# Attention outputs placed by feature with DMAs and divided late, in a two-layer kernel on one Trainium2 core

## Chip, cores and metric

The kernel runs on one core of a Trainium2 chip. The metric is the device time of one execution in microseconds (us), median of the runs shown. The engines are named as in the profile: PE (TensorE matmul; PEld its weight loads), DVE (VectorE), ACT (ScalarE), POOL (GpSimd) and SP (SyncE, here a queue that only issues DMAs and waits). All inputs and the output are float32.

## The reference, cut to what matters

The input has 2 sequences of 1024 tokens with 128 features. Two layers follow each other: attention plus a state scan with a mixture of experts, then a causal latent attention with a second mixture of experts. Both attentions have 16 heads of 8 features. What is computed around the change is, for each head:

```python
# layer 0, full attention (4 key/value heads, one for each group of 4 query heads)
p = softmax(q @ k.T / sqrt(8)); out = p @ v             # out: tokens x 8, 16 heads side by side = 128 features
# layer 1, causal
attn = jnp.where(causal_mask[None, None], -jnp.inf, attn)
attn = jax.nn.softmax(attn, axis=-1)
y = jnp.einsum('bhtl,hld->bhtd', ctx, v_eff).transpose(0, 2, 1, 3).reshape(B, T, C)
x = x + y                                               # the residual
```

The softmax's denominator is the row sum of the exponentials. The kernel computes numerators (exponentials times v) and denominators (exponentials times one) and divides afterwards.

## The kernel before

Activations are held by feature: 128 features on the partitions, 2048 tokens in the free direction, as four blocks of 512 columns. The program is a chain of blocks with a barrier between: preparation of the scan, attention 0 (`hybrid_attention`, profile 90 to 515 us), the scan (515 to about 1170 us), `latent_layer` (merge, gated layer and experts of layer 0, and attention 1, whose units run from 1320 to 1575 us), and the experts of layer 1 to the end. A block ends when each of its engines has come to its end.

Both attentions are the one function `attention`. A unit is one group of 4 heads of one sequence; there are 8 units (`UNITS`), in the order given by `units`. In a unit the queries are in two halves `qb` of 512. It has NE slots, 32 in attention 0 and 24 in attention 1; a slot handles one tile of 128 keys for two heads: PE computes their transposed scores (`exp_unit`), ACT takes the exponential of two 128x512 tiles (in attention 1 they are cut by the causal mask), and PE multiplies with v (`pv_quad`), into one bank `out_acc`. The rows of `out_acc` are 32 for each head: 8 numerators, one denominator (the column of ones in `vst`), and 23 unused. Half 0 ends with slot MID - 1 (MID is 16 in attention 0 and 8 in attention 1).

Beside that a first pass runs ahead in the same slots: PE computes scores (`max_unit`), DVE takes their row maxima (`take_max`, L581 in attention 0, L578 in attention 1), `combine` splits the maxima in three bf16 parts (L591 to L595), PE turns them to rows (`turn_max`), ACT copies the rows (L514), and SP's `rows` places them with three DMAs (L310, the tile `attn_mrow`) in the query operand `attn_qa`. The exponentials of half 0 of unit i wait for `rows(i, 0)`, those of half 1 for `rows(i, 1)` (`mrow_sent`). The planner's slots (worked out from its code) are: attention 0, `turn_max(i, 1)` in slot 12 for slot 16, `turn_max(i + 1, 0)` in slot 28 for slot 0 of the next unit; attention 1, `turn_max(i, 1)` in slot 3 for slot 8, `turn_max(i + 1, 0)` in slot 12 for slot 0 of the next unit. In the last unit there is no unit ahead, so the first pass ends early (slot 10 of attention 0, slot 1 of attention 1).

SP also loads the operands of unit i + 2 (`load_part`, three parts of six DMAs, L266 and L299), each paced by a wait on a slot of unit i. In attention 0 SP ends with `sync_third`, which loads 3.5 MB for the scan back into SBUF (ct, bt and twelve pieces of xparts) and waits for them; before, it comes right after the last `rows(7, 1)`.

When a half is done, the output goes: ACT copies `out_acc` to SBUF (`out_copy`, L519, tile `attn_osb`); PE turns it to token-major in 32 weight loads and 32 matmuls (`turn_out`, L362 with `attn_osb`, into the bank `turned`); DVE takes the reciprocal of 16 denominators per token row and multiplies (`out_norm`, L604 and L608), into a token-major buffer that is `ssm_in`. `turn_out(i - 1, 1)` stands in slot 3 (attention 0) or 5 (attention 1) of unit i (`OUT_AT`), `turn_out(i, 0)` in slot MID + 3. After the last unit PE turns the whole buffer back to features (L503, 4 x 4 tiles of 128x128), and ACT copies it to `attn_t` (attention 0, L563) or DVE adds it to x (attention 1, L638).

Of the kernel before, what the change touches and what calls it, by code (L numbers as in the profile page):

```python
# [14 lines left out]
T = BATCH * SEQ  # L15
# [117 lines left out]
def sl(i, w=BLK):  # L133
    return slice(i * w, (i + 1) * w)
# [6 lines left out]
def attention(k, tag, q_lin, k_lin, k_heads, v, causal, attn_t, front, units, tok=None, residual=False,  # L141
# [18 lines left out]
    with ExitStack() as ctx:  # L160
# [8 lines left out]
        osb = k.sb(f"{tag}_osb", [128, BLK], F32, ctx)  # L169
        rden = k.sb(f"{tag}_rden", [128, 4, 4], F32, ctx)  # L170
        if tok is None:
            tok = k.sb(f"{tag}_tok", [128, T], F32, ctx)
        attn_tok = tok[:, :].rearrange("p (t m) -> p t m", m=HEADS * HD)
# [56 lines left out]
        OUT_AT = 5 if causal else 3  # L230
# [17 lines left out]
        oturned = k.sem(f"{tag}_oturned")  # L248
        normed = k.sem(f"{tag}_normed")
        own_dve = k.sem(f"{tag}_own_dve")  # L250
        own_norm = k.sem(f"{tag}_own_norm")
        final_turned = k.sem(f"{tag}_final_turned")
        final_copied = k.sem(f"{tag}_final_copied")
# [15 lines left out]
        with nc.Block() as block:  # L269
            @block.sync  # L270
            def _(sp):
# [40 lines left out]

                front.sync_first(sp, load_part)
# [8 lines left out]
                for i in range(UNITS):  # L322
                    rows(i, 1)
                    if i + 2 < UNITS:
                        load_part(i + 2, 0)
                    if causal and i + 1 < UNITS:
                        rows(i + 1, 0)
                    if i + 2 < UNITS:
                        load_part(i + 2, 1)
                        load_part(i + 2, 2)  # L330
                    if not causal and i + 1 < UNITS:
                        rows(i + 1, 0)
                front.sync_third(sp)

            @block.gpsimd
            def _(pool):
# [9 lines left out]
                for i in range(2):  # L346
                    nc.gpsimd.memset(vst[i][:, :, :, :], 0.0).then_inc(vst_cleared, 1)
                    pool.wait_ge(vst_cleared, 2 * i + 1)
                    nc.gpsimd.memset(vst[i][:, :, :, HD:HD + 1], 1.0).then_inc(vst_cleared, 1)
# [5 lines left out]
            def _(pe):  # L355
# [23 lines left out]
                def turn_max(i, half):  # L379
# [3 lines left out]
                    if i > 0:  # L383
                        pe.wait_ge(normed, 2 * i - 1 + (half if not causal else 0))
                    if causal and half == 1:
                        pe.wait_ge(mrow_ready[0], i + 1)
                    for t in range(4):
# [45 lines left out]
                def turn_out(i, qb):  # L433

                    pe.wait_ge(osb_ready, 2 * i + qb + 1)
                    pe.wait_ge(normed, 2 * i + qb)

                    if qb == 0:
                        pe.wait_ge(mrow_ready[1], i + 1)
                    elif i + 1 < UNITS:  # L440
                        pe.wait_ge(mrow_ready[1 if causal else 0], i + 2)
                    for t in range(4):
                        last = quad(turned[:, sl(t, TILE)], osb[:, sl(t, TILE)], k.m("ident"))
                    last.then_inc(oturned, 1)

# [8 lines left out]
                def body(i):  # L454
                    for s in range(NE):
# [22 lines left out]
                        if s == OUT_AT and i > 0:  # L478
                            turn_out(i - 1, 1)
                        if s == MID + 3:  # L480
                            turn_out(i, 0)
# [14 lines left out]
                turn_out(UNITS - 1, 1)  # L496

                pe.wait_ge(normed, 16)
                for n in range(NBLK):
                    if n >= 2:  # L500
                        pe.wait_ge(final_copied, n - 1)
                    for t in range(4):
                        last = nc.tensor.matmul(k.bank[n % 2][:, sl(t, TILE)], attn_tok[:, 4 * n + t, :],  # L503
                                                k.m("ident"), start=True, stop=True)
                    last.then_inc(final_turned, 1)
# [2757 lines left out]
```

## Time and profile before

| | us |
|---|---|
| median of 3 runs | 1913.33 (1907.16 to 1920.68) |
| profiled execution | 1904.06 |
| its span | 1902.3 |
| PE busy over the span | 1624.3 (85%) |
| DVE busy | 1478.2 (78%) |
| ACT busy | 1350.6 (71%) |
| POOL busy | 882.9 (46%) |

All times of the rows below are from the start of the span of the profiled execution. A busy share is an average over stages with different limits; what matters here is which engine has no gap in the two attentions, and what follows what where they end.

### The profile page before, as it was taken

How to read it: one execution, taken by the hardware profiler on the slowest of the kernel's cores; microseconds unless marked ns; L12 is line 12 of the kernel's file. 1: busy time of each engine (PE TensorE's matmuls, PEld its weight loads, DVE VectorE, ACT ScalarE, POOL GpSimd, SP SyncE). 2: the span in 40 equal slices, each digit the busy share in tenths (PEclk: the TensorE clock that was granted, in tenths of full speed). 3: DMA queues.
4: the chain of work that ended last, by engine and by line, in shares of the span. 5: the costliest groups of instructions: out<-in, count | busy, mean ns of one | idle time of the engine just before them, and what ended most of it. 6: DMA issues, size and time to landing. Idle time of an engine off the chain costs nothing. (4 is left out here: it accounts for less than half of the span.)

```text
span 1902.3 us, 45877 instructions
## 1 busy us (share of the span) xinstructions
PE 1624.3 (85%) x17422; PEld 857.2 (45%) x17422; DVE 1478.2 (78%) x1729; ACT 1350.6 (71%) x2673; POOL 882.9 (46%) x526
## 2 busy tenths in 40 slices
PE   6789999999887766676767669998999998999996
PEld 2235555555344434344444433433556555344442
DVE  3588899999299999999999975447888845556457
ACT  4418888888799999989999953443777773654443
POOL 0166666666099999999999971000000002000000
PEclk8769999999999899898888989996999999999998
DMA  2344444443489988888898842031222100000000
GB/s 118 119 154 151 161 154 159 158 155 136 142 325 313 319 309 299 313 289 306 295 319 300 299 148 88 13 72 41 46 39 46 30 4 18 0 1 0 0 6 17
DMA packets 82504, 278.86 MB, mean 147 GB/s; under 512 B 11159, under 2 KB 11954, under 8 KB 81311
## 3 DMA queue, kind: packets, MB, share of 16 engines
q1 hardware_dynamic: 68223, 225.67, 35.7%
q0 software_dynamic: 13824, 50.34, 6.7%
q8 instruction: 124, 2.03, 0.5%
q10 hardware_dynamic: 288, 0.45, 0.1%
q14 instruction: 45, 0.37, 0.1%
HBM read 214.72 MB, written 61.21 MB: 145 GB/s over the span
## 5 line engine op out<-in xcount | busy, mean ns | idle before, releaser
L1680 POOL TENSOR_TENSOR hc<-st,ct 128x1024 f32<-128x1024 f32 x256 | 596.5, 2369 | 9.8 <-DVE st L1626 8.4
L1626 DVE TENSOR_TENSOR_SCAN st<-da,banks 128x1024 f32<-128x1024 f32 x256 | 561.9, 2265 | 13.5 <-ACT da L1583 5.5
L528 ACT ACTIVATE attn_probs<-banks 128x512 f32<-128x512 f32 (+3 forms) x640 | 325.0, 534 | 91.3 <-PE banks L362 74.6
L362 PE MATMUL banks<-attn_qa,attn_ka 75*32 75x512 bf16 (+3 forms) x3584 | 346.7, 363 | 9.3 <-DMA attn_qa<-attn_mrow 2.9
L581 DVE TENSOR_REDUCE attn_mx<-banks 128x1 f32<-128x1024 f32 x256 | 309.9, 1223 | 29.0 <-PE banks L362 16.7
L1591 ACT ACTIVATE ut<-b_turned,mats 128x128 f32<-128x128 f32 x1024 | 311.7, 388 | 1.7
L362 PE MATMUL banks<-attn_ka,attn_qa 72*32 72x512 bf16 (+3 forms) x3584 | 289.5, 379 | 17.5 <-DVE attn_mx L578 10.8
L1583 ACT ACTIVATE da<-dt,mats 128x1024 f32<-128x1024 f32 x256 | 282.7, 1139 | 22.6 <-DVE st L1626 17.4
L1508 PE MATMUL banks<-hc,onecols 128*32 128x512 f32 x1024 | 155.9, 686 | 95.5 <-POOL hc L1680 73.8
L759 POOL TENSOR_TENSOR made_ahead<-b_turned,x_turned 128x1024 f32<-128x1024 f32 x96 | 184.2, 1918 | 89.4 <-DVE attn_mparts L595 70.8
L578 DVE CUSTOM_DVE_ANT_0 banks<-banks,attn_maskwide 128x128 f32<-128x128 f32 (+7 forms) x256 | 191.2, 775 | 31.4 <-PE banks L362 27.8
L1483 PE MATMUL banks<-mats,ut 128*128 128x128 f32 x1024 | 167.3, 300 | 45.7 <-DVE st L1626 34.8
L425 PE MATMUL banks<-attn_probs,attn_vst 128*32 128x256 f32 (+3 forms) x2560 | 180.2, 349 | 1.6 <-ACT attn_probs L528 0.5
L528 ACT ACTIVATE centred_squares<-banks 128x512 f32<-128x512 f32 x256 | 150.6, 596 | 37.0 <-PE banks L362 27.4
L1483 PEld LDWEIGHTS banks<-mats,ut 128*128 128x128 f32 x1024 | 132.5, 150 | 83.7 <-ACT ut L1591 53.4
L362 PEld LDWEIGHTS banks<-attn_qa,attn_ka 75*32 75x32 bf16 x3584 | 101.0, 94 | 133.1 <-ACT attn_probs L528 47.4
L362 PEld LDWEIGHTS banks<-attn_ka,attn_qa 72*32 72x32 bf16 x3584 | 108.0, 99 | 96.3 <-DVE attn_mx L578 23.8
L2627 PE MATMUL banks<-hid_m,ew 128*128 128x512 f32 x320 | 146.4, 592 | 0.0
L1491 PEld LDWEIGHTS banks<-mats,ua 128*128 128x128 f32 x768 | 98.7, 160 | 104.9 <-issue 60.1
L1491 PE MATMUL banks<-mats,ua 128*128 128x128 f32 x768 | 124.0, 314 | 8.0 <-DVE st L1626 7.8
L3066 POOL MEMSET route_tok<- 128x128 bf16 x1 | 0.2, 205 | 272.9 <-issue 272.9
L425 PEld LDWEIGHTS banks<-attn_probs,attn_vst 128*32 128x32 f32 x2560 | 78.3, 110 | 33.7 <-issue 4.2
(447 smaller groups left out, 1938.5 us busy)
## 6 DMA issues: line engine op xcount, KB each, us to landing
dt<-dt_rows SPq DMA_DIRECT2D x256, 512.0 KB, 5.6
ahead<-made_ahead POOLq DMA_DIRECT2D x96, 512.0 KB, 3.3
ua<-ahead SPq DMA_DIRECT2D x96, 512.0 KB, 6.0
attn_qa<-q_lin SPq DMA_DIRECT2D x144, 64.0 KB
attn_ka<-k_lin SPq DMA_DIRECT2D x72, 64.0 KB
moe_w<-in_moe_w SPq DMA_DIRECT2D x2, 2048.0 KB, 9.8
mats<-in_mats SPq DMA_DIRECT2D x1, 2988.5 KB, 13.0
xparts_kept<-xparts_lin SPq DMA_DIRECT2D x3, 512.0 KB, 4.7
```

The source lines that it names most:

```text
L362: last = nc.tensor.matmul(out[sl(t, 32), :], lhs[:, sl(t, 32)], rhs, start=start, stop=True, skip_group_check=True)
L425: last = nc.tensor.matmul(out_acc[32 * j:32 * j + 32, cols], vstage[:, kt, kj(j), :], probs[(kt_slot + j // 2) % 4][:, j % 2, cols],  star ...
L528: nc.scalar.activation(probs[s % 4][:, jj, c0:BLK], scores_exp[jj][:, c0:BLK], ACT.Exp, scale=scale).then_inc(probs_ready, 1)
L578: nc.vector.tensor_tensor_reduce(out, out, mask_wide[:, SEQ - w:SEQ], 1.0, -BIG, ALU.add, ALU.max, mx[:, qt, j:j + 1]).then_inc(max_taken, 1)
L581: nc.vector.reduce_max(mx[:, qt, j:j + 1], out, AX.X).then_inc(max_taken, 1)
L759: nc.gpsimd.tensor_tensor(stage[:, :, :], scan.b_turned[:, 8 * b:8 * b + 8, :], x, ALU.mult)\
L1483: ins = nc.tensor.transpose(pair[:, i // 4, sl(i % 4, TILE)], buf[:, i, :], k.m("ident"))
L1491: ins = nc.tensor.transpose(pair[:, i // 4, sl(i % 4, TILE)], ua[q % 3][:, i, :], k.m("ident"))
L1583: nc.scalar.activation(da[n % 4][:, :], dt[n % 4][:, :], ACT.Exp, scale=a_now[:, g, jp:jp + 1])\
L1591: nc.scalar.activation(ut[TURNED.index(n) % 2][:, i, :], b_turned[:, 8 * b + i, :], ACT.Copy, scale=x_now[:, i, g, jp:jp + 1]).then_inc(ut ...
L1626: nc.vector.tensor_tensor_scan(st[n % 4][:, :], da[n % 4][:, :], pair[:, :, :].rearrange("p h t -> p (h t)"), 0.0, ALU.mult, ALU.add).then ...
L1680: nc.gpsimd.tensor_tensor(hc[n % 8][:, :], st[n % 4][:, :], ct[:, b * SEQ:(b + 1) * SEQ], ALU.mult)\
```

## The change

The turned output is gone: no `turn_out`, no `out_norm`, no token-major buffer, no final turning, and no `rden`.

- `vst` now has ones in 8 columns per head and not in one, so `out_acc` has per head 8 numerators and 8 equal denominators on 16 of its 32 rows.
- `out_copy` writes one of two buffers `osb[qb]`, and waits only for the DMAs that read this buffer one unit earlier (`out_sent[qb]`).
- SP's new `out_rows(i, qb)` waits for the copy and issues 8 DMAs of 8 partitions x 512 float32: for each of the 4 heads, numerators to `attn_t` and denominators to `den_t` (the same memory as the token-major buffer before, `ssm_in`). So there are 16 more DMAs for each unit on SP's queue.
- In attention 0 the order of SP in iteration i is: `out_rows(i-1, 1)`, `rows(i, 1)`, `load_part(i+2, 0)`, `out_rows(i, 0)`, `load_part(i+2, 1)`, `load_part(i+2, 2)`, `rows(i+1, 0)`. In attention 1 it is: `rows(i, 1)`, `out_rows(i-1, 1)`, `load_part(i+2, 0)`, `out_rows(i, 0)`, `rows(i+1, 0)`, `load_part(i+2, 1)`, `load_part(i+2, 2)`. After the last unit `out_rows(7, 1)` comes ahead of `sync_third`.
- DVE's new `divide(b, qb)` works on a whole block of 128x512 by feature: a reciprocal in place, a multiplication, and in attention 1 the addition to x. The two blocks of the sequence that is finished first are divided from slot 12 of the last unit on, the third from slot MID + 7, the fourth after the last `out_rows` has landed.
- `turn_max` waits for ACT's copy of the rows before (`mrow_ready`) where it waited for DVE's `normed`.

```diff
--- before.py
+++ after.py
...
@@ -166,11 +166,7 @@
         mrow = k.sb(f"{tag}_mrow", [12, 2, BLK], BF16, ctx)
-        osb = k.sb(f"{tag}_osb", [128, BLK], F32, ctx)
-        rden = k.sb(f"{tag}_rden", [128, 4, 4], F32, ctx)
-        if tok is None:
-            tok = k.sb(f"{tag}_tok", [128, T], F32, ctx)
-        attn_tok = tok[:, :].rearrange("p (t m) -> p t m", m=HEADS * HD)
+        osb = [k.sb(f"{tag}_osb{i}", [128, BLK], F32, ctx) for i in range(2)]
         ident_b = k.sb(f"{tag}_identb", [128, 128], BF16, ctx)
@@ -227,7 +223,6 @@
         turn_at = [done_half[0] + 2, done_half[1] + 2]
-        OUT_AT = 5 if causal else 3
         LOAD_SLOT = [5, 14, 18] if causal else [13, 19, 23]
...
@@ -310,6 +303,17 @@
+                def out_rows(i, qb):
+
+                    g, b = units[i]
+                    cols = slice(b * SEQ + qb * BLK, b * SEQ + (qb + 1) * BLK)
+                    sp.wait_ge(osb_ready, 2 * i + qb + 1)
+                    for j in range(4):
+                        rows = sl(4 * g + j, HD)
+                        sp.dma_start(attn_t[rows, cols], osb[qb][32 * j:32 * j + HD, :]).then_inc(out_sent[qb], 16)
+                        sp.dma_start(den_t[rows, cols], osb[qb][32 * j + HD:32 * j + 2 * HD, :])\
+                            .then_inc(out_sent[qb], 16)
+
                 front.sync_first(sp, load_part)
@@ -320,9 +324,14 @@
                 for i in range(UNITS):
+                    if i > 0 and not causal:
+                        out_rows(i - 1, 1)
                     rows(i, 1)
+                    if i > 0 and causal:
+                        out_rows(i - 1, 1)
                     if i + 2 < UNITS:
                         load_part(i + 2, 0)
+                    out_rows(i, 0)
                     if causal and i + 1 < UNITS:
@@ -330,6 +339,7 @@
                         rows(i + 1, 0)
+                out_rows(UNITS - 1, 1)
                 front.sync_third(sp)
@@ -346,7 +356,7 @@
                     pool.wait_ge(vst_cleared, 2 * i + 1)
-                    nc.gpsimd.memset(vst[i][:, :, :, HD:HD + 1], 1.0).then_inc(vst_cleared, 1)
+                    nc.gpsimd.memset(vst[i][:, :, :, HD:2 * HD], 1.0).then_inc(vst_cleared, 1)
                     pool.wait_ge(vst_cleared, 2 * i + 2)
@@ -380,10 +390,10 @@
-                    if i > 0:
-                        pe.wait_ge(normed, 2 * i - 1 + (half if not causal else 0))
-                    if causal and half == 1:
+                    if half == 1:
                         pe.wait_ge(mrow_ready[0], i + 1)
+                    elif i > 0:
+                        pe.wait_ge(mrow_ready[1], i)
                     for t in range(4):
@@ -429,19 +439,6 @@
                         last.then_inc(pv_done, 2)
-
-                def turn_out(i, qb):
-
-                    pe.wait_ge(osb_ready, 2 * i + qb + 1)
-                    pe.wait_ge(normed, 2 * i + qb)
-
-                    if qb == 0:
-                        pe.wait_ge(mrow_ready[1], i + 1)
-                    elif i + 1 < UNITS:
-                        pe.wait_ge(mrow_ready[1 if causal else 0], i + 2)
-                    for t in range(4):
-                        last = quad(turned[:, sl(t, TILE)], osb[:, sl(t, TILE)], k.m("ident"))
-                    last.then_inc(oturned, 1)
@@ -475,10 +472,6 @@
                             pv_quad(*products_with_v, 1)
-                        if s == OUT_AT and i > 0:
-                            turn_out(i - 1, 1)
-                        if s == MID + 3:
-                            turn_out(i, 0)
@@ -493,16 +486,6 @@
                     pv_quad(UNITS - 1, NE - 2, vst[1], part)
-                turn_out(UNITS - 1, 1)
-
-                pe.wait_ge(normed, 16)
-                for n in range(NBLK):
-                    if n >= 2:
-                        pe.wait_ge(final_copied, n - 1)
-                    for t in range(4):
-                        last = nc.tensor.matmul(k.bank[n % 2][:, sl(t, TILE)], attn_tok[:, 4 * n + t, :],
-                                                k.m("ident"), start=True, stop=True)
-                    last.then_inc(final_turned, 1)
@@ -515,8 +498,9 @@
                     act.wait_ge(pv_done, NE * i + half_end[qb] + 1)
-                    act.wait_ge(oturned, 2 * i + qb)
-                    nc.scalar.copy(osb[:, :], out_acc[:, :]).then_inc(osb_ready, 1)
+                    if i > 0:
+                        act.wait_ge(out_sent[qb], 128 * i)
+                    nc.scalar.copy(osb[qb][:, :], out_acc[:, :]).then_inc(osb_ready, 1)
@@ -558,9 +542,6 @@
                 out_copy(UNITS - 1, 1)
-                for n in range(NBLK if not residual else 0):
-                    act.wait_ge(final_turned, n + 1)
-                    nc.scalar.copy(attn_t[:, sl(n)], k.bank[n % 2][:, :]).then_inc(final_copied, 1)
@@ -596,18 +577,21 @@
-                def out_norm(i, qb):
-
-                    dve.wait_ge(oturned, 2 * i + qb + 1)
-                    dve.wait_ge(normed, 2 * i + qb)
-                    tv = turned[:, :].rearrange("p (t j c) -> p t j c", t=4, j=4)
-                    link(nc.vector.reciprocal(rden[:, :, :], tv[:, :, :, 8]), 2 * i + qb + 1, own_norm)
-                    g, b = units[i]
-                    t0 = b * QT + 4 * qb
-                    dst = attn_tok[:, t0:t0 + 4, sl(g, 32)].rearrange("p t (j c) -> p t j c", j=4)
-                    nc.vector.tensor_tensor(dst, tv[:, :, :, 0:8],
-                                            rden[:, :, :].unsqueeze(3).to_broadcast([128, 4, 4, 8]), ALU.mult)\
-                        .then_inc(normed, 1)
+                def divide(b, qb):
+
+                    unit = max(i for i, u in enumerate(units) if u[1] == b)
+                    blk = 2 * b + qb
+                    dve.wait_ge(out_sent[qb], 128 * (unit + 1))
+                    num, den = attn_t[:, sl(blk)], den_t[:, sl(blk)]
+                    taken[0] += 1
+                    link(nc.vector.reciprocal(den, den), taken[0], inverted)
+                    ins = nc.vector.tensor_tensor(num, num, den, ALU.mult)
+                    if residual:
+                        link(ins, taken[0], divided)
+                        nc.vector.tensor_tensor(k.x[:, sl(blk)], k.x[:, sl(blk)], num, ALU.add)
+
+                taken = [0]
+                last_b = units[UNITS - 1][1]
@@ -618,10 +602,10 @@
                                 combine(i + 1, 0)
-                        if s == OUT_AT and i > 0:
-                            out_norm(i - 1, 1)
-                        if s == MID + 3:
-                            out_norm(i, 0)
+                        if i == UNITS - 1 and s in (12, 13):
+                            divide(1 - last_b, s - 12)
+                        if i == UNITS - 1 and s == MID + 7:
+                            divide(last_b, 0)
@@ -632,11 +616,7 @@
                     body(i)
-                out_norm(UNITS - 1, 1)
-                for n in range(NBLK if residual else 0):
-                    dve.wait_ge(final_turned, n + 1)
-                    nc.vector.tensor_tensor(k.x[:, sl(n)], k.x[:, sl(n)], k.bank[n % 2][:, :], ALU.add)\
-                        .then_inc(final_copied, 1)
+                divide(last_b, 1)
```

## Rows read from the trace of the kernel before

**Rows 1.** Busy time by stretch (stretch, length, PE, PEld, DVE, ACT, POOL, clock, DMA share, GB/s)
```profile
200.00:250.00 50.00, 49.02 (x924) 29.61 (x920) 45.56 (x50) 43.29 (x76) 31.91 (x26) 1.00 0.41 152
...
1400.00:1450.00 50.00, 48.03 (x1228) 28.84 (x1217) 43.69 (x117) 37.99 (x84) 0.00 (x0) 1.00 0.28 43
```

**Rows 2.** Timeline of PE in unit 1 of attention 0 (start, us, instruction, idle before)
```profile
195.29 1.08 PE L362 MATMUL banks<-mats,attn_osb 128*32 128x128 f32 x32
196.16 0.43 PE L362 MATMUL banks<-attn_qa,attn_ka 75*32 75x512 bf16 x4
...
206.25 0.40 PE L362 MATMUL banks<-attn_ka,attn_qa 72*32 72x512 bf16 x4 [0.54 <-DVE attn_mx L581]
```

**Rows 3.** Timeline of DVE in the same stretch
```profile
196.43 0.26 DVE L604 RECIPROCAL attn_rden<-banks 128x16 f32<-128x16 f32 x1 [0.32 <-PE banks L362]
196.72 0.29 DVE L608 TENSOR_TENSOR ssm_in<-banks,attn_rden 128x128 f32<-128x128 f32 x1
197.06 9.05 DVE L581 TENSOR_REDUCE attn_mx<-banks 128x1 f32<-128x1024 f32 x7
```

**Rows 4.** Timeline of attention 1, unit 1: PE and SP's queue
```profile
1354.68 0.27 PE L388 MATMUL banks<-attn_identb,attn_mparts 128*12 128x128 bf16 x2
...
1356.18 1.81 SPq L310 DMA_DIRECT2D attn_qa<-attn_mrow  x3
...
1357.58 1.04 PE L362 MATMUL banks<-mats,attn_osb 128*32 128x128 f32 x32
...
1360.02 0.40 PE L362 MATMUL banks<-attn_qa,attn_ka 75*32 75x512 bf16 x4
```

**Rows 5.** Timeline of attention 0, unit 0 into unit 1: ACT, SP's queue, PE
```profile
169.92 0.58 ACT L519 COPY attn_osb<-banks 128x512 f32<-128x512 f32 x1
...
185.89 1.89 SPq L310 DMA_DIRECT2D attn_qa<-attn_mrow  x3
...
189.79 0.40 PE L362 MATMUL banks<-attn_qa,attn_ka 75*32 75x512 bf16 x4 [0.34 <-DMA attn_qa<-attn_mrow]
```

**Rows 6.** Instructions by line (count: duration in ns, min/median/max, first and last start)
```profile
L299 SPq DMA_DIRECT2D attn_qa<-q_lin x144: 263/298/1432, 97.5 to 1504.3; - x144
...
L310 SPq DMA_DIRECT2D attn_qa<-attn_mrow x96: 572/578/772, 137.8 to 1546.0; - x96
...
L604 DVE RECIPROCAL attn_rden<-banks x32: 256/258/259, 173.5 to 1569.1; 128x16 f32<-128x16 f32 x32
...
L595 DVE TENSOR_TENSOR attn_mparts<-attn_mres,attn_mparts x32: 174/176/177, 136.4 to 1543.3; 128x16 bf16<-128x16 f32 x32
```

**Rows 7.** Timeline of the end of attention 0 and the start of the scan
```profile
485.34 0.45 SPq L732 DMA_DIRECT2D ct<-ct_kept  x1
...
507.82 0.59 ACT L519 COPY attn_osb<-banks 128x512 f32<-128x512 f32 x1 [1.19 <-PE banks L425]
...
515.02 0.35 SPq L1461 DMA_DIRECT2D dt<-dt_rows  x1
```

**Rows 8.** Busy time by stretch there, columns as in rows 1
```profile
495.00:500.00 5.00, 4.58 (x72) 1.68 (x76) 0.00 (x0) 4.62 (x10) 0.00 (x0) 1.00 0.90 181
500.00:505.00 5.00, 4.65 (x76) 1.53 (x68) 0.00 (x0) 4.70 (x10) 0.00 (x0) 1.00 0.01 4
515.00:519.00 4.00, 3.49 (x14) 1.79 (x14) 0.17 (x1) 2.94 (x12) 0.00 (x0) 1.00 0.63 219
519.00:522.40 3.40, 0.00 (x0) 0.00 (x0) 2.15 (x1) 1.71 (x2) 0.00 (x0) 1.00 1.02 388
522.60:529.00 6.40, 5.39 (x21) 3.87 (x21) 5.87 (x4) 6.40 (x17) 4.96 (x5) 0.50 1.03 409
```

**Rows 9.** Timeline of the end of attention 1 and what follows
```profile
1567.34 0.59 ACT L519 COPY attn_osb<-banks 128x512 f32<-128x512 f32 x1 [0.55 <-PE banks L425]
...
1573.79 0.69 DVE L638 TENSOR_TENSOR x<-x,banks 128x512 f32<-128x512 f32 x1 [0.21 <-PE banks L503]
1574.76 0.30 SPq L3092 DMA_DIRECT2D alpha<-in_eb_rows  x1
1574.80 3.67 PE L2509 MATMUL banks<-x,mats 128*128 128x512 f32 x8 [1.04 <-PEq L269]
```

More of the change, by code:

```diff
@@ L138, with attention @@
 K_ORDER = [0, 1, 2] * 3
-def attention(k, tag, q_lin, k_lin, k_heads, v, causal, attn_t, front, units, tok=None, residual=False,
+def attention(k, tag, q_lin, k_lin, k_heads, v, causal, attn_t, front, units, den_t, residual=False,
               probs=()):
@@ L247, in attention @@
         osb_ready = k.sem(f"{tag}_osb_ready")
-        oturned = k.sem(f"{tag}_oturned")
-        normed = k.sem(f"{tag}_normed")
+        out_sent = [k.sem(f"{tag}_out_sent{i}") for i in range(2)]
         own_dve = k.sem(f"{tag}_own_dve")
-        own_norm = k.sem(f"{tag}_own_norm")
-        final_turned = k.sem(f"{tag}_final_turned")
-        final_copied = k.sem(f"{tag}_final_copied")
+        inverted = k.sem(f"{tag}_inverted")
+        divided = k.sem(f"{tag}_divided")
         vst = [k.sb(f"{tag}_vst{i}", [128, QT, nk, 32], F32, ctx) for i in range(2)]
```

## The prediction

> **What bounds the kernel now.** I read the busy time by stretch first, since only the two attentions are touched. In both, PE is busy 48 to 49 of 50 us, DVE 44 to 46, ACT 38 to 43, at full clock [rows 1]. Busy PE can be overlapping records, so the second view is PE's timeline around a turned output. There `turn_out` starts at 195.29 and the next scores at 196.16: it takes 0.87 us of PE's stream, and the work before and behind it stands without a gap [rows 2]. The third view is DVE at the same place: it waits 0.32 us for the turning, spends 0.63 us on `out_norm` (196.43 to 197.06), and then takes seven maxima in 9.05 us, 1.29 each, where PE delivers one a slot [rows 3]. PE's next wait for DVE is 0.54 us at 206.25, ten microseconds later and at a `combine` [rows 2]. So PE sets the pace, and DVE makes up its delay.
>
> Two more places matter. Where a half's exponentials begin, PE may wait for the max rows: three DMAs, issued from 185.89 to 187.78, let PE on at 189.79, so they land 2.0 us after their issue, and PE had waited 0.34 us [rows 5]. And each attention has an end in which one thing follows another: the last output copy, turning, norm, final turning, final copy [rows 7, 9].
>
> **In the units.** There are 32 outputs (the count of L604 [rows 6]): 15 in each attention beside other work, and one at each end.
>
> Attention 0: no `turn_out` lies between a `turn_max` and the slot that needs its rows (12 to 16, 28 to 0; the outputs are in slots 3 and 19). So each gives back its 0.87 us: 15 x 0.87 = 13.1 us saved.
>
> Attention 1: the output of slot MID + 3 = 11 lies free: 8 x 0.87 = 7.0 us saved. That of slot 5 lies inside the chain from `turn_max` in slot 3 to slot 8: turned at 1354.68, rows issued 1356.18 to 1357.99, plus 2.0 us = 1360.0, and slot 8 starts at 1360.02 [rows 4]. PE would be there 0.87 us earlier and wait for the same DMAs. What is late next is the max rows, and the stall that goes comes back whole. I take nothing for these seven; the other bound is 7 x 0.87 = 6.1 us.
>
> DVE's 0.63 us an output go too. They bring nothing more as long as PE sets the pace; a bound for the case that they do is among the rivals. ACT's copy is the same. The ones in 8 columns cost nothing: the matmul has 32 columns per head anyway.
>
> **On SP's queue.** 16 DMAs a unit come in. A price for this form is not in the trace. The load of 8 partitions (L299) takes SP 0.30 us, the small one from SBUF to SBUF (L310) 0.58 [rows 6]; three of these take 1.81 to 1.89 [rows 4, 5], so there is 0.04 between. The new ones have 8 partitions on both sides and equal shapes, nearest to L299: 0.34 apiece, 2.7 us for eight; the other bound is 0.61, 4.9 us. Behind `out_rows(i, 0)` two parts of loads (12 x 0.34 = 4.1 us) and `rows(i+1, 0)` are queued, whose lateness PE feels at once (it waits already). The copy is done at 170.50 and those rows are issued at 185.89 [rows 5]: 15.4 us for 4.9 + 4.1 at most. Hidden. `out_rows(i-1, 1)` starts near slot 2, ten slots ahead of `rows(i, 1)`; in attention 1 it stands behind it. ACT's wait for `out_sent` looks one unit back, 30 us or more: nothing.
>
> **The end of attention 0.** Before: copy done at 508.41, scan starts at 515.02, 6.6 us [rows 7]. `sync_third` began at 485.34 [rows 7], and its transfers filled the DMA engines until 500 (share 0.90, then 0.01 [rows 8]): 14.7 us, hidden under unit 7. Now it is queued behind `out_rows(7, 1)`, which waits for the last copy. So nothing hides it: 2.7 + 14.7 + 0.3 for leaving the block = 17.7 us, 11.1 us lost. This is the step that a look at PE alone misses. If the transfers held the rate of their first megabytes, they would take some 10 us (bound 6 lost); with 0.61 a DMA 13.3 are lost. DVE's last division runs beside.
>
> **The end of attention 1.** Before: copy done 1567.93, next stage 1574.76, 6.8 us [rows 9]. Now: 2.7 of issue, 2.0 to land, reciprocal, multiplication 0.69, addition 0.69, 0.1 between, 0.3 to leave. The reciprocal of 128x512 is not in the trace. That of 16 elements takes 258 ns where a TENSOR_TENSOR of 16 takes 176 [rows 6], and one of 512 takes 690 [rows 9], so the latter is 1.04 ns an element on 160 ns. If the rest of the reciprocal is per element, it is 98/16 = 6.1 ns, 3.3 us for 512. Bounds: 0.8 us (the 82 ns are fixed), 8.3 us (all 258 ns scale). I take 3.3, between them, for the extra over a TENSOR_TENSOR is large for so few elements. Sum 9.8 us, 3.0 lost (0.5 to 8, or 2.2 more with slow DMAs).
>
> The Trainium skill (VectorE: DVE Perf Modes, "First, the fixed hardware budget") says that the reciprocal is an iterative divide with a repeat count of 8. At its 0.96 GHz an estimate from that is 4.3 us, 1 us more than by the row; no row here shows a long one. The three earlier divisions of each attention lie where DVE has no maxima left.
>
> **The clock.** PE was idle from 519.0 to 522.4, and the granted clock of the next stretch is 0.50, that is 1.2 GHz [rows 8]. After the change PE is idle for 18 and 10 us at the two ends, where before it was turning. The scan then begins with 3.5 us of PE work at full clock in its first 4 us [rows 8], the experts with 3.67 us for eight matmuls [rows 9]. At half clock each takes up to 3.5 us more. In the scan PE shares the path with the first loads: 1.5 us; the experts start on PE: 2.0 us; bounds 0 and 3.5 each.
>
> The Trainium skill (TensorE: Matmul & The Clock Gate, "Part 1") speaks against this change for the same reason: an idle array falls back to half rate and must earn the full one again. It agrees with the row; without it the sum would be 3.5 us lower.
>
> **Sum.** -13.1 - 7.0 + 11.1 + 3.0 + 1.5 + 2.0 = -2.5 us. Against the profiled execution's 1904.06 that is 1901.6. The median of the runs shown is 9 us above that execution, so on its scale 1913.3 - 2.5 = 1910.8. About 1% (19 us) is what a measurement can tell from no change.
>
> **Rivals.**
> A. Both engines' stalls add up (faster). If PE's 0.87 and DVE's 0.63 us come back one behind the other in all 30 outputs, 45 us are saved, less 17.6 at the ends: 27 us, 1886. For it: DVE is busy 91% in attention 0, the first pass has only two banks, and PE does wait for DVE, 0.54 us. Against it: PE runs ten microseconds without a gap behind an output [rows 2].
> B. SP's queue holds up the max rows (slower). If a new DMA holds SP until it has landed, 0.6 + 2.0 us, eight take 21, and 21 + 4 is 10 us over the 15.4 of rows 5, in 7 units: 67 us slower, 1978. It decides from 1.4 us a DMA on. For it: the longest L299 took 1.43 us. Against it: no median is above 0.6.
> C. The ends cost little (loads at the fast rate, short reciprocal, no clock loss) and slot 5 pays (faster only if all of it holds): -2.5 - 5 - 2.5 - 3.5 - 6.1 = -19.6 us, 1893.7; any part of it stays within 1%.
> D. The ends cost all they can: +2.2 x 2, +5, +3.5: 1924, still within 1%.
>
> **Chances.** The forecast with the milder parts of C and D 0.76, A or all of C (faster) 0.13, B or something like it, as rows that land later behind the new DMAs, 0.11. Range: C and D with a run's scatter, 1893 to 1927; A and B are left out with most of their 2 in 10. Faster by over 1% 0.13, within 1% 0.76, slower 0.11.
>
> **What would show it.** In units of attention 0 the period falls by 1.7 us, in those of attention 1 by 0.9, not 1.7, with new waits for `attn_mrow` at slot 8. `sync_third` starts after the last copy, with PE, ACT and POOL idle for some 15 us. The long reciprocal's row gives its price. Wrong I am if the maxima set the pace, if the waits at slot 8 don't appear, or if the loads of `sync_third` are faster than before.

## The result and the profile after

The changed kernel takes 1923.88 us (median of 14 runs, 1917.02 to 1929.92), the kernel before 1907.24 us on the same chip (14 runs, 1901.15 to 1920.68). The ratio is 1.0086, 95% interval 1.0070 to 1.0102: 16.4 us slower, 13.4 to 19.5. Forecast was a change of -2.5 us. So the time went the other way, by an amount that the measurement can tell: its interval is 6 us wide, where the prediction had taken 19 us as the least that can be told.

To see where, both traces are cut at the same instructions: the first and the last output copy of each attention, the first load of the scan, the first load of the stage behind the scan, the first load of the experts' stage.

| stretch (us) | before | after | difference | forecast |
|---|---|---|---|---|
| attention 0, first to last output copy | 337.9 | 326.7 | -11.2 | -13.1 |
| last copy to the scan's first load | 7.2 | 21.8 | +14.6 | +11.1 |
| scan | 624.5 | 626.8 | +2.3 | +1.5 |
| scan to first output copy | 191.6 | 190.9 | -0.7 | 0 |
| attention 1, first to last output copy | 236.2 | 242.5 | +6.3 | -7.0 |
| last copy to the experts' first load | 7.4 | 12.3 | +4.9 | +3.0 |
| experts | 327.5 | 329.9 | +2.4 | +2.0 |

The rows for it, by tile, of the kernel after (line, engine, count, ns min/median/max, first and last start); attention 0 first, then attention 1, then all output DMAs:

```profile
L503 ACT COPY attn_osb<-banks x16: 580/580/593, 171.1 to 497.8; 128x512 f32<-128x512 f32 x16
...
L503 ACT COPY attn_osb<-banks x16: 580/588/593, 1337.3 to 1579.8; 128x512 f32<-128x512 f32 x16
...
L313 SPq DMA_DIRECT2D attn_t<-attn_osb x128: 624/625/1486, 171.8 to 1584.5; - x128
L314 SPq DMA_DIRECT2D ssm_in<-attn_osb x128: 624/625/1561, 172.5 to 1585.1; - x128
```

And the kernel before, attention 1, whose last copy is that of [rows 9]:

```profile
L519 ACT COPY attn_osb<-banks x16: 579/583/592, 1331.1 to 1567.3; 128x512 f32<-128x512 f32 x16
```

One row has the wrong sign, attention 1; the others lie within 3.5 us of their forecast. The waits of PE between 1325 and 1600 us say what is new there (line, what it waited for: us in total, times, longest):

```profile
PE banks L372 <- DMA attn_qa<-q_lin: 14.8, 5, 5.2
PE banks L372 <- ACT attn_probs L512: 2.3, 9, 0.4
...
PE banks L372 <- DMA attn_qa<-attn_mrow: 0.2, 1, 0.2
```

PE waits for the loads of q, not for the max rows that the prediction watched. One of the five waits, and SP's queue in the 30 us ahead of it (timeline of after: start, us, instruction):

```profile
1428.33 1.82 SPq L303 DMA_DIRECT2D attn_qa<-attn_mrow  x3
1430.19 0.67 SPq L313 DMA_DIRECT2D attn_t<-attn_osb  x1
...
1434.92 0.62 SPq L314 DMA_DIRECT2D ssm_in<-attn_osb  x1
1435.64 0.41 SPq L259 DMA_DIRECT2D attn_ka<-k_lin  x1
...
1437.12 0.65 SPq L259 DMA_DIRECT2D attn_ka<-k_lin  x2
1437.82 0.65 SPq L313 DMA_DIRECT2D attn_t<-attn_osb  x1
...
1442.52 0.62 SPq L314 DMA_DIRECT2D ssm_in<-attn_osb  x1
1443.18 1.85 SPq L303 DMA_DIRECT2D attn_qa<-attn_mrow  x3
1445.08 0.46 SPq L259 DMA_DIRECT2D attn_ka<-k_lin  x1
...
1449.11 0.27 SPq L292 DMA_DIRECT2D attn_qa<-q_lin  x1
...
1458.29 0.30 PE L372 MATMUL banks<-attn_ka,attn_qa 72*32 72x128 bf16 x4 [2.63 <-DMA attn_qa<-q_lin]
```

The queue has no hole from 1428.33 to 1449.4: rows, eight outputs, six loads, eight outputs, rows, twelve loads. Eight outputs take 1430.19 to 1435.54, 5.35 us, that is 0.667 us from one issue to the next. Before, it had a hole of 5.5 us at this place, and the twelve loads began behind it:

```profile
1424.42 1.37 SPq L266 DMA_DIRECT2D attn_ka<-k_lin  x2
1431.29 1.82 SPq L310 DMA_DIRECT2D attn_qa<-attn_mrow  x3
1433.15 0.46 SPq L266 DMA_DIRECT2D attn_ka<-k_lin  x1
...
1441.19 0.26 SPq L299 DMA_DIRECT2D attn_qa<-q_lin  x1
```

The last loads then have to drain, that is, their bytes have to arrive. The busy time of that stretch, with clock and DMA share (columns as in [rows 1]), after:

```profile
1446.00:1456.00 10.00, 9.32 (x260) 5.28 (x252) 8.65 (x18) 7.46 (x20) 0.00 (x0) 1.00 0.55 81
1456.00:1462.00 6.00, 3.71 (x63) 2.77 (x67) 2.37 (x14) 2.20 (x6) 0.00 (x0) 0.57 0.03 3
```

and before:

```profile
1434.00:1444.00 10.00, 9.90 (x265) 5.94 (x260) 8.29 (x16) 7.62 (x18) 0.00 (x0) 1.00 0.53 81
1444.00:1450.00 6.00, 5.25 (x148) 3.05 (x140) 5.49 (x17) 4.63 (x11) 0.00 (x0) 1.00 0.03 5
```

In both kernels the twelve loads take about ten microseconds at 81 GB/s, issued within 8.3 us before and within 4.3 after. What moved is when they begin. Counted from the output copy ahead of them (1426.02 before, 1434.96 after), the first is issued at 7.1 us before and at 10.1 after, and they are drained at 18 us before and at 21.3 after. PE is ready for them at 20.7 us (1458.29 less the wait of 2.63) and goes on at 23.3, 2.0 us behind the drain. With the drain of before, those same 2.0 us would have let PE on at 20.0: the slack was 0.7 us, and the change took 3.3. The second row of after shows a price on top: from 1456 to 1462 the granted clock is 0.57 on average, partly the 1.2 GHz level.

The two ends. Attention 0, SP's queue and DVE:

```profile
497.81 0.58 ACT L503 COPY attn_osb<-banks 128x512 f32<-128x512 f32 x1 [1.19 <-PE banks L435]
...
498.42 0.62 SPq L313 DMA_DIRECT2D attn_t<-attn_osb  x1
...
503.76 0.45 SPq L712 DMA_DIRECT2D ct<-ct_kept  x1
...
504.72 5.88 SPq L716 DMA_DIRECT2D xparts<-xparts_kept  x12
505.10 3.35 DVE L587 RECIPROCAL ssm_in<-ssm_in 128x512 f32<-128x512 f32 x1 [12.91 <-DMA ssm_in<-attn_osb]
508.49 0.69 DVE L588 TENSOR_TENSOR attn_t<-attn_t,ssm_in 128x512 f32<-128x512 f32 x1
519.60 0.35 SPq L1441 DMA_DIRECT2D dt<-dt_rows  x1
```

Outputs 5.3 us, then 15.8 us from `ct` to `dt`; DVE has been done for 10.4 us when the scan starts. Attention 1:

```profile
1587.13 3.35 DVE L587 RECIPROCAL ssm_in<-ssm_in 128x512 f32<-128x512 f32 x1 [8.79 <-DMA ssm_in<-attn_osb]
...
1592.19 0.30 SPq L3072 DMA_DIRECT2D alpha<-in_eb_rows  x1
```

### The profile page after: what moved, and what is told of

It is laid out like the page before. It is cut to its first block and busy times, and to the rows that moved or that the text cites. A ratio compares the mean times of both kernels' runs of the same rounds, so it can differ in the third digit from the quotient of the medians.

```text
span 1922.1 us, 43838 instructions
## 1 busy us (share of the span) xinstructions
PE 1586.5 (83%) x16334; PEld 816.6 (42%) x16334; DVE 1493.7 (78%) x1681; ACT 1348.4 (70%) x2669; POOL 882.4 (46%) x526
## 5 line engine op out<-in xcount | busy, mean ns | idle before, releaser
L1660 POOL TENSOR_TENSOR hc<-st,ct 128x1024 f32<-128x1024 f32 x256 | 596.2, 2366 | 13.3 <-DVE st L1606 11.7
L372 PE MATMUL banks<-attn_qa,attn_ka 75*32 75x512 bf16 (+3 forms) x3584 | 349.6, 367 | 11.8 <-DMA attn_qa<-attn_mrow 4.4
L372 PE MATMUL banks<-attn_ka,attn_qa 72*32 72x512 bf16 (+3 forms) x3584 | 289.5, 381 | 30.1 <-DMA attn_qa<-q_lin 14.8
L559 DVE CUSTOM_DVE_ANT_0 banks<-banks,attn_maskwide 128x128 f32<-128x128 f32 (+7 forms) x256 | 190.9, 778 | 51.3 <-PE banks L372 48.4
L1463 PE MATMUL banks<-mats,ut 128*128 128x128 f32 x1024 | 160.5, 298 | 52.9 <-DVE st L1606 45.1
L1471 PEld LDWEIGHTS banks<-mats,ua 128*128 128x128 f32 x768 | 94.5, 155 | 103.6 <-issue 57.4
L1471 PE MATMUL banks<-mats,ua 128*128 128x128 f32 x768 | 119.1, 305 | 8.3 <-DVE st L1606 7.8
## 6 DMA issues: line engine op xcount, KB each, us to landing
moe_w<-in_moe_w SPq DMA_DIRECT2D x2, 2048.0 KB, 10.1
mats<-in_mats SPq DMA_DIRECT2D x1, 2988.5 KB, 12.9
```

What stands on the lines that cost most here:

```text
L372: last = nc.tensor.matmul(out[sl(t, 32), :], lhs[:, sl(t, 32)], rhs, start=start, stop=True, skip_group_check=True)
L559: nc.vector.tensor_tensor_reduce(out, out, mask_wide[:, SEQ - w:SEQ], 1.0, -BIG, ALU.add, ALU.max, mx[:, qt, j:j + 1]).then_inc(max_taken, 1)
L1463: ins = nc.tensor.transpose(pair[:, i // 4, sl(i % 4, TILE)], buf[:, i, :], k.m("ident"))
L1471: ins = nc.tensor.transpose(pair[:, i // 4, sl(i % 4, TILE)], ua[q % 3][:, i, :], k.m("ident"))
L1660: nc.gpsimd.tensor_tensor(hc[n % 8][:, :], st[n % 4][:, :], ct[:, b * SEQ:(b + 1) * SEQ], ALU.mult)\
```

## Experiments

The question: is attention 1 slower because of the issues in SP's queue (theory), or because of the new transfers themselves, or the bunched loads? And what are the ends and the clock worth? Times are medians, ratios go against the kernel before on the same chip.

**One attention at a time.** Two kernels hold both versions of `attention`, and call the new one for attention 0 alone, or for attention 1 alone.

```
-        attention(k, "attn1", ...)        # e1; in e2 the call of attn0
+        attention_old(k, "attn1", ...)
```

> Attention 0 as changed, attention 1 as before. If the loss is the sum of two separate ones, this kernel has the loss that the two traces show up to the end of the scan: the scan starts 4.6 us later (units 10 us shorter, end 14.6 us longer) and its start costs 2.3 us more at the half clock, so about 7 us above before, and nothing in attention 1. If the new order of attention 1 alone made the kernel slower, this one is 0 to 3 us above before.

Measured 1910.03 us, ratio 1.0022 (1.0001 to 1.0042): +4.2 us. Attention 0 takes 325.5 us between its copies (-12.4), its end 21.8 (+14.6); attention 1 236.3, as before.

> Attention 1 as changed, attention 0 as before. Separate losses: from the first output copy to the last 6.4 us more, end 5 us more, start of the experts 2.4 us more, so about 13 us above before; waits of PE for the q_lin loads of some 15 us in all. If instead the loss of attention 1 were carried over from attention 0 (later start, other state of the queues), it would be below 5 us here.

Measured 1923.91 us, ratio 1.0093 (1.0074 to 1.0112): +17.7 us. Attention 1 takes 243.1 us (+6.9), its end 12.3 (+4.9), with 12.9 us of waits for q_lin in four places (four other traces with this attention 1 have 11.8 to 15.0). So the loss is attention 1's. The two do not add up well (21.9 for 16.4 measured, with intervals of 3 to 4 us each), and in e2 some 6 us lie outside of attention 1; e8 below says what to think of them.

**Loads ahead of outputs.** The bytes, the DMAs and the queue stay; only the order in attention 1 changes.

```
                     rows(i, 1)
-                    if i > 0 and causal:
-                        out_rows(i - 1, 1)
                     if i + 2 < UNITS:
                         load_part(i + 2, 0)
-                    out_rows(i, 0)
+                    if i > 0 and causal:
+                        out_rows(i - 1, 1)
+                    if not causal:
+                        out_rows(i, 0)
                     if causal and i + 1 < UNITS:
                         rows(i + 1, 0)
                     if i + 2 < UNITS:
                         load_part(i + 2, 1)
                         load_part(i + 2, 2)
+                    if causal:
+                        out_rows(i, 0)
```

> The changed kernel, but in attention 1 SP issues the loads of unit i+2 ahead of the output DMAs: out_rows(i-1, 1) behind load part 0 and out_rows(i, 0) behind part 2. The same DMAs, the same bytes. Theory Q (the queue): 16 issues of 0.67 us stand ahead of the loads, which are issued late and bunched; with the order turned, PE's 15 us of waits for q_lin go, and first to last copy of attention 1 falls from 242.6 to about 228 us: some 14 us faster than the changed kernel, 1910. Theory B (bytes): the new transfers take the DMA engines from the loads; then the waits stay near 15 us and the time too. On the max rows of slot 8: if they land 1.15 us after their issue as in the one unit of the changed kernel's trace without a load wait, PE waits there 0.3 us a unit; if 2.0 us, 0.9.

Measured 1906.71 us, ratio 1.0003 (0.9984 to 1.0023): 16 us gained over the changed kernel, and the kernel before is reached. The copies span 226.2 us, 16.3 less than after (one unit took 31.4 and not 29.7, with 1.2 us in it in which PE waited for nothing that the profile shows), and no wait for q_lin is left in PE's list (between 1325 and 1600 us):

```profile
PE banks L375 <- DVE attn_mx L562: 2.6, 10, 0.3
PE banks L375 <- ACT attn_probs L515: 2.3, 9, 0.4
...
PE banks L375 <- DMA attn_qa<-attn_mrow: 0.3, 1, 0.3
```

**Fewer bytes, fewer issues, another queue.** Three ways to lighten the outputs of attention 1. First the bytes: each DMA sends 16 of its 512 columns.

```
-  sp.dma_start(attn_t[rows, cols], osb[qb][32 * j:32 * j + HD, :])
+  sp.dma_start(attn_t[rows, thin(cols)], osb[qb][32 * j:32 * j + HD, 0:WIDE])     # 16; den_t alike
```

> The changed kernel, but each output DMA of attention 1 carries 16 of its 512 columns (8 partitions x 64 bytes), same count, same place in SP's order. It leaves most of attention 1's output unplaced. Theory Q: issue costs stay near 0.62 us, the loads are as late as before, PE's waits for q_lin stay near 15 us. Theory B: with 1/32 of the bytes the waits go.

Measured 1923.32 us (a single run), the copies span 242.2 us, the waits for q_lin are 15.0 us. The issue costs what it did:

```profile
L318 SPq DMA_DIRECT2D attn_t<-attn_osb x64: 624/625/1506, 1337.3 to 1583.4; - x64
```

One thirty-second of the bytes changes neither the price of an issue nor the time. Then the issues: the denominators' DMAs left out (so what is divided by is not the denominators, and half of the bytes go too; e4 says that bytes are not it).

```
+  if not causal:
       sp.dma_start(den_t[rows, cols], osb[qb][32 * j + HD:32 * j + 2 * HD, :]).then_inc(out_sent[qb], 16)
```

> The changed kernel, whose attention 1 leaves out the denominators' DMAs (so its output is divided by what the scan left in that buffer): four output DMAs a half instead of eight, nothing else. Theory (what delays the loads of qa is the number of issues in SP's queue ahead of them, 0.667 us each): a unit loses 8 x 0.667 = 5.3 us of the 10.7, the loads land 5 us earlier, and the waits for q_lin, at most 5.2 us each (14.8 in all), go or shrink to 0 to 2 us in all; from attention 1's first copy to its last 242.6 becomes 227 to 229. Rival (the loads are late for another reason: the twelve of a unit, bunched, drain slowly at 8 to 9 us from the last issue): they are as bunched as before, the waits shrink by less than half, 235 to 240.

Measured 1906.30 us (a single run); 223.9 us between the copies, no wait of PE for q_lin. The twelve loads of the same unit are issued over 8.1 us here, over 4.3 in after, and drain in the same ten to eleven (1434 to 1445). That speaks against the rival: their bunching changes nothing, and a drain of that length is harmless if it starts in time, here 18.5 us after the copy at its end. Last the queue: `out_rows` of attention 1 in POOL's program, behind `gpsimd_third`.

```
+  for i in range(UNITS if causal else 0):
+      for qb in range(2):
+          pool.wait_ge(osb_ready, 2 * i + qb + 1)
+          for j in range(4):
+              pool.dma_start(attn_t[rows, cols], ...); pool.dma_start(den_t[rows, cols], ...)
```

> The changed kernel, whose attention 1 sends its outputs (all 128 DMAs of it, the same bytes) from POOL's queue, where nothing stands; SP's queue holds rows and loads alone, as in the kernel before. Theory (SP's queue): no wait for q_lin, unit period 29.8 as where no wait falls, 226 to 228 us from the first copy to the last. Rival (the transfers themselves hinder the loads or the rows on the DMA engines): waits remain, 235 us and up. The end of attention 1 depends on what an issue costs on POOL, 10 to 15 us.

Measured 1909.98 us (a single run); 224.8 us between the copies, no wait for q_lin. The same transfers hinder no load here. The end of attention 1 grew to 15.6 us, and not by the issues (0.50 us each):

```profile
1572.11 0.69 DVE L604 TENSOR_TENSOR x<-x,attn_t 128x512 f32<-128x512 f32 x1
1577.49 0.30 SPq L3085 DMA_DIRECT2D alpha<-in_eb_rows  x1
```

4.7 us pass between DVE's last instruction and the next stage, where the changed kernel has 0.3. What POOL does in them the trace does not show.

**The end of attention 0.** The issues of `sync_third` go ahead of the last outputs, and only its wait stays behind them.

```
-                out_rows(UNITS - 1, 1)
                 front.sync_third(sp)
+                out_rows(UNITS - 1, 1)
+                front.sync_last(sp)          # sp.wait_ge(self.scan_in, 16 * 14)
```

> The changed kernel with one edit in attention 0's end: the loads of the scan's inputs (the issues of ct, bt and xparts) stand in SP's queue ahead of the last unit's second half of outputs, and only the wait for them stands behind it. In the changed kernel those issues start at 503.8 us, behind the eight output DMAs, and the first dt load follows at 519.4, while the reciprocal and the product are done at 509.2. Theory (the exposed part of attention 0's end is the loads behind the outputs, 519.4 - 509.2 = 10.2 us): from the last copy to dt 21.8 becomes 11.5 to 12.5 us, and the time 1923.9 becomes 1913 to 1915. Rival (the loads only share the memory's bandwidth with something that goes on anyway, or push the output DMAs back by as much as they take, 6.8 us of issues): from the copy to dt 17 to 19 us, time 1919 to 1921.

Measured 1914.99 us, ratio 1.0043 (1.0019 to 1.0067): 8 us less than after, give or take 5. The scan's first load follows DVE's product by 0.3 us, 12.4 us after the last copy began (499.46):

```profile
507.48 3.35 DVE L588 RECIPROCAL ssm_in<-ssm_in 128x512 f32<-128x512 f32 x1 [13.73 <-DMA ssm_in<-attn_osb]
510.87 0.69 DVE L589 TENSOR_TENSOR attn_t<-attn_t,ssm_in 128x512 f32<-128x512 f32 x1
...
511.83 0.36 SPq L1444 DMA_DIRECT2D dt<-dt_rows  x1
```

**The clock at the two starts.** 90 and 56 matmuls that nobody reads, behind the last product with V of attention 0 and of attention 1.

```
                     pv_quad(UNITS - 1, NE - 2, vst[1], part)
+                for _ in range(56 if causal else 90):
+                    filler(turned[:, :])
```

> The changed kernel with TensorE kept busy through both ends: 90 matmuls of 512 columns that nobody reads behind attention 0's last product with V, 56 behind attention 1's. In the changed kernel TensorE's granted clock is 0.50 (the 1.2 GHz level) when the scan and the experts start, after 22 and 12 us of nothing. Theory (the clock costs what the first instructions show: the scan's ninth scan instruction is 0.7 us later against its start than before, the experts take 329.9 for 327.5): the scan's first 25 us 0.7 us shorter, the experts 2.4 us shorter, together 3.1, time about 1920.8, and the scan's other 2.5 us, lost at its middle (842 to 851 us, clock 0.50 there too), stay. Rival (the loss at the scan's middle is a late effect of the same clock at its start): the scan 624.5 again, time about 1918.3. Rival (the start clock isn't what costs): 1923 to 1925.

Measured 1923.86 us, ratio 1.0115 (1.0075 to 1.0156): no gain, in an interval of 8 us to either side that could not show the 3.1 expected. The profiled span is 2.2 us shorter than after, with experts of 327.3 us. At the scan this run tests nothing: the fill ended 3.3 us too soon, and the scan's first matmuls ran at half rate all the same:

```profile
520.39 3.78 PE L1498 MATMUL banks<-mats 128*128 128x512 f32 x4 [3.30 <-DVE mats L1590]
```

**The kernel before, profiled once more.** Nothing edited.

> The kernel before once more, unchanged, with a profile. The scan took 624.5 us in its first profile, and 626.8 to 627.9 in the five profiles since: of the changed kernel, of two variants of it, and also of the one whose attention 0 is the old one. About 2.5 us of it arise at the scan's middle, where TensorE waited 3.1 us (before, clock 1.00 after it) or 3.1 to 4.3 us (the others, clock 0.50 after it). Theory (the level that the clock has there differs from one execution to the next, the change has no part in it): this run's scan takes 627 or 624.5, and may well show the 0.50. Rival (something of the change does it): 624.5 again, with 1.00.

Measured 1916.62 us, span 1914.8. Its stretches, in the order of the table above: 337.9, 7.2, 625.2, 187.3, 235.9, 7.4, 332.5; its first output copy starts at 181.4 us instead of 169.9. So the attentions and their ends repeat within 0.3 us, while what leads to the first copy moved by 11.5 us, the stretch ahead of attention 1 by 4.3 and the experts by 4.9. The scan's 625.2 lies between the 624.5 and 627 that were asked about; it is 627.9 in e2, whose attention 0 is the old one. Differences of 2 to 3 us in the whole scan or the whole experts between single traces are therefore no evidence. At the scan's middle DVE's wait for PE, 1.91 us in the first trace of before and 4.4 in after's, is 3.5 here: it moves without any change.

**All mended.** The order of e3, that of e5, the last four denominators' DMAs of each attention from ACT's queue, and 40 matmuls of fill per end; then the same without fill.

```
+  act.wait_ge(osb_ready, 2 * UNITS)          # behind out_copy(UNITS - 1, 1)
+  for j in range(4):
+      act.dma_start(den_t[sl(4 * g + j, HD), cols], osb[1][32 * j + HD:32 * j + 2 * HD, :]).then_inc(out_sent[1], 16)
```

> The changed kernel with four edits: in attention 1 the next unit's loads stand ahead of the output DMAs in SP's queue (alone: span 1905.1); the scan's input loads ahead of the last outputs of attention 0 (expected -9.5); the last four denominator DMAs of each attention from ACT's queue, idle by then (8 issues x 0.667 become 4, -2.7 at each end); 40 matmuls of fill in each end for the clock (-3.1). If these add: 1923.9 - 17.2 - 9.5 - 5.3 - 3.1 = 1888.8, range 1885 to 1893, so 14 to 22 us below the kernel before (1907.2). Rival (the memory's bandwidth or the transfers' latency, not the issues, set the two ends): ends 14 and 11 us, time 1894 to 1898.

Measured 1890.44 us, ratio 0.9928 (0.9903 to 0.9953). Attention 1 225.3 us, ends 10.0 and 10.4 us. Measured again beside the one without fill:

> The fully mended kernel with its fill once more, beside the one without it on one chip: 1890.4 in its first measurement, ratio to the kernel before 0.9928. Expected 1889 to 1892, ratio 0.991 to 0.994, and 3 us under the one without fill (theory) or within 1 us of it (rival).

Measured 1893.20 us, ratio 0.9936 (0.9910 to 0.9961).

> The fully mended kernel (1890.4 us: loads ahead of outputs, the scan's input loads ahead of the last outputs, the last denominators from ACT's queue) without the 40 + 40 matmuls of fill. Theory (fill is worth the clock at the two starts, 0.7 us at the scan and 2.5 at the experts): 3 us slower than with it, 1893.5. Rival (at ends of 10 us each the clock doesn't fall, or it comes back at once): the same within 1 us.

Measured 1891.10 us, ratio 0.9909 (0.9887 to 0.9931). Without fill the scan's first four matmuls take 3.71 us, with it 1.99, and the scans then last 625.1 and 625.6 us. The experts' first eight matmuls show the same, after first, then the mended kernel without and with fill (before had 3.67 [rows 9]):

```profile
1592.24 5.93 PE L2489 MATMUL banks<-x,mats 128*128 128x512 f32 x8 [12.46 <-PEq L262]
1561.77 6.24 PE L2505 MATMUL banks<-x,mats 128*128 128x512 f32 x8 [10.33 <-PEq L262]
1558.54 3.67 PE L2507 MATMUL banks<-x,mats 128*128 128x512 f32 x8 [1.87 <-PEq L262]
```

So the clock did fall, the fill did hold it, and at the start of the experts that is worth 2.3 to 2.6 us of PE's time. The times do not show it: the medians are 2.1 us apart the other way, and each has an interval of 4 to 5 us to either side. Whether the 2 us last to the end stays open. The experts take 327.0 to 328.8 us in the three traces with fill and 329.3 to 333.6 in the eight that have the new end of attention 1 without it, but with the old end before's own two traces have 327.5 and 332.5, and e1 has 327.4. The version without fill beats both kernels: 17 us below the kernel before, 33 below the changed one.

## Why the prediction was wrong, step by step

- **What bounds the kernel: right.** PE sets the pace in the units, and its stall comes back: between output copies two apart, a unit without a wait lost 1.7 us in attention 0 (45.8 to 44.1) and 1.8 in attention 1 (31.5 to 29.7 or 29.8), twice the 0.87 of a turned output.
- **Attention 0's units: right.** -13.1 forecast, -11.2 here, -12.4 in e1.
- **Attention 1's slot 5: wrong, to the good.** I took the rows to land 2.0 us after their issue, as in [rows 5], and so gave the output in slot 5 nothing. In after, the rows are issued from 1361.45 to 1363.27, and slot 8 starts at 1364.42 after a wait of 0.31 us: landed 1.15 us after the last issue. Without waits for loads attention 1 gains 10.0 to 12.3 us (e3, e10, e9), not 7.0. The expected waits for `attn_mrow` are there and short: in e3, e9 and e10 PE's weight loads wait for them seven times, 2.4 to 2.8 us in all, where 0.87 a unit was expected.
- **"On SP's queue ... Hidden": the step that failed.** Two things were wrong in it. The price: of the two bounds, 0.34 us (the load from memory with as many partitions) and 0.61 (SBUF to SBUF, four partitions to one), I took the lower, by the partitions. It is 0.667, near the row of the same kind of transfer. And the check: I compared 15.4 us of room in attention 0 [rows 5] and did not do it for attention 1, whose units are 31.5 us, not 46, and whose two blocks of outputs stand between loads. There the sum is 16 x 0.667 = 10.7 us of new issues; they delayed the twelve loads by 3 us, where the slack was 0.7. The wait is for loads due a unit later, and I had asked only after the rows. What the waits cost is 17.7 us, from -11.4 (e10) to +6.3. 14.8 of it are the waits themselves; the other 2.9 I put down to the lower clock behind them, which no run separates. e3, e9 and e10 each take the loss away, e4 does not.
- **Rival B** had the right resource and the wrong victim and threshold: it has SP's queue hold up the max rows from 1.4 us a DMA on. The loads were held up at 0.667.
- **End of attention 0: mechanism right, one term short.** 2.7 + 14.7 + 0.3 = 17.7 us from the end of the copy, measured 21.2: outputs 5.3 for 2.7, and 15.8 for 15.0 of loads and leaving. e5 shows that 9.4 of them were the loads' place in the queue.
- **End of attention 1: right but for the same term.** 9.8 forecast, 11.8 measured: issues 5.3 for 2.7, landing 1.4 for 2.0. The reciprocal of 512 is 3.35 us, 3.3 forecast by scaling the row of 16. The Trainium skill (VectorE: DVE Perf Modes, "First, the fixed hardware budget") with its repeat count of 8 had given an estimate of 4.3; the measurement decides for 3.35.
- **Clock: seen at the starts, not in the time.** +3.5 forecast. The half rate is there: four matmuls take 3.78 us at the scan's start, 1.99 before, and eight take 5.93 at the experts', 3.67 before. The Trainium skill (TensorE: Matmul & The Clock Gate, "Part 1") says that an idle array falls back to half rate. The traces agree. At the scan little of it lasts: its ninth scan instruction came 0.7 us later against the start than before, for 1.5 forecast. At the experts PE's next line of work came 2.3 us later, for 2.0 forecast. Medians with and without fill show neither.

By traces the two attentions, their ends and the two starts sum to -11.2 + 14.6 + 6.3 + 4.9 + 0.7 + 2.3 = 17.6 us, for 16.4 measured (13.4 to 19.5). With the issue priced at 0.667 and all else as forecast the sum would have been about +2.7; the other 13.3 us are attention 1's, +6.3 for -7.0. That the measured 1923.9 lies in the range of 1893 to 1927, and on the 1924 of rival D, is luck: D had neither the waits nor a before of 1907 us, but a longer reciprocal, which did not come.

Open: why an issue from SBUF to SBUF costs SP twice one from memory with as many partitions. It is not the bytes (e4); the number of partitions was not varied.

## What to carry to other kernels

A queue that is free half of the time is not free at every place: for each block of new issues, ask which transfer behind it is due first, in each stage where the loop runs, at that stage's period, and count the drain of that transfer as well as its issue. Put what is due soonest and drains longest ahead of what nobody waits for; here one reordering was worth 16 us and another 8, together more than the 16 that the change had cost. And price an issue by a row with the same two ends before one of the same shape: here 0.61 was near and 0.34 was not.

## What the runs showed of the hardware

- A DMA from SBUF to SBUF, 8 partitions to 8, holds SP's queue for 0.624 us, 0.667 from one to the next, with 512 columns or 16 alike; from POOL's queue it is 0.497. Loads from memory cost SP 0.298 (8 partitions) and 0.438 (`xparts`, 32 partitions).
- Twelve loads of 64 KB, eight partitions each, drain in 10 us (81 GB/s at a DMA share of 0.53 to 0.55), whether issued within 4.3 us or within 8.3.
- In e10, where the outputs went from POOL's queue, 4.7 us passed between the last work of attention 1 and the next stage, instead of 0.3. That is one trace, and its cause is open.
- After a wait of PE of 3.2 us the granted clock was 0.56 from 1426 to 1430, and around one of 2.6 us 0.57 from 1456 to 1462. After 12.5 us of idle PE eight matmuls took 5.93 us instead of 3.67.
- PE went on 2.0 us after the last bytes of its loads had arrived (1456.3 to 1458.29).
- RECIPROCAL of 128x512 f32: 3.35 us, 6.5 ns a column, against 0.69 us for a TENSOR_TENSOR of that size.
